# Three edits in a six-stage transformer kernel: local stages with a chain one tick shorter, norms finished in their own tick, half copies on GpSimd, and the distance stage's output made inside its units

## The reference

```python
x = x + 0.5 * _L0_ffn_ref(_layernorm(x), ...)
x = x + _L0_attn_ref(_layernorm(x), ...)        # "distance": softmax(-|q_i - q_j|^2 / sqrt(8)), 16 heads of 8
x = x + 0.5 * _L0_ffn_ref(_layernorm(x), ...)
x = x + 0.5 * _L1_ffn_ref(_layernorm(x), ...)   # "local": 2 layers, below
x = x + _L1_attn_ref(_layernorm(x), ...)        # causal attention, 16 heads of 64
x = x + 0.5 * _L1_ffn_ref(_layernorm(x), ...)   # "local" again
# one local layer (8 heads of 64, windows of 64 rows):
h = shift_token(x)                # columns 64..127 come from the row before
q, k, v = split(h @ wqkv)
q = l2norm(q) * qs; k = l2norm(k) * ksc
q, k = rotary_xpos(q, k)
o = local_attention(q, k, v)      # softmax over own and preceding window, masked
x = x + o @ wo
h = shift_token(x); h = layernorm(h) * lg + lb
a, g = split(h @ w1 + b1)
x = x + (a * gelu(g)) @ w2 + b2
```

## Time and profile before

| | |
|---|---|
| median of 3 runs | 3463.14 us (3461.46 to 3471.44) |
| the profiled execution: time, span | 3464.99 us, 3463.2 us |
| busy in the span: PE, ACT, DVE, POOL | 3167.9 (91%), 2201.9 (64%), 1959.3 (57%), 1441.8 (42%) us |
| distance units, then their output block | 138 to 630 us, 630 to 648 us |
| first local stage | about 729 to 1480 us |
| causal stage between | to about 2700 us |
| second local stage | 2706 to 3463 us |
| granted TensorE clock, mean | 0.971 of 2.4 GHz |

### The profile page before, as it was taken

One profiled execution on the slowest core, in us unless ns is written; L12 is line 12 of the kernel. 1 busy time (PEld: TensorE's weight loads), 2 busy tenths in 40 slices (PEclk: granted clock), 3 DMA queues, 4 the chain that ended last, 5 costly groups with the idle time before them and its releaser, 6 DMA issues. The chain is left out here.

```text
span 3463.2 us, 74421 instructions
## 1 busy us (share of the span) xinstructions
PE 3167.9 (91%) x26438; PEld 1948.0 (56%) x26564; DVE 1959.3 (57%) x4017; ACT 2201.9 (64%) x3837; POOL 1441.8 (42%) x1765
## 2 busy tenths in 40 slices
PE   7799999769999999769999999999999599999996
PEld 5322222436666666546666666666666366666664
DVE  4200000338777777645565655655655587777774
ACT  2599999436766666545555555555555366666664
POOL 1100000037677766423333333333333376777673
PEclk9799999989999999989999999999999799999999
DMA  1122222101111111000000000000000111111111
GB/s 33 30 39 39 36 39 33 67 16 40 35 39 40 39 35 36 21 13 8 6 9 6 9 6 6 9 6 6 9 6 5 25 41 35 38 39 38 37 34 37
DMA packets 121646, 90.38 MB, mean 26 GB/s; under 512 B 79985, under 2 KB 99057, under 8 KB 121329
## 3 DMA queue, kind: packets, MB, share of 16 engines
q1 hardware_dynamic: 121168, 87.70, 11.6%
q10 hardware_dynamic: 288, 0.13, 0.0%
HBM read 17.52 MB, written 2.10 MB: 6 GB/s over the span
## 5 line engine op out<-in xcount | busy, mean ns | idle before, releaser
L1893 POOL TENSOR_SCALAR e<-e,inv 128x768 f32<-128x768 f32 (+7 forms) x512 | 376.8, 749 | 762.0 <-DVE inv L1785 762.0
L1855 ACT ACTIVATE e<-e,nmax 128x768 f32<-128x768 f32 (+7 forms) x512 | 395.6, 773 | 429.4 <-DVE e L1780 426.9
L1780 DVE TENSOR_SCALAR_CACHE_REDUCE e<-slot 128x768 f32<-128x768 f32 (+7 forms) x512 | 376.2, 754 | 247.9 <-PE slot L1669 247.9
L661 ACT ACTIVATE e<-slot 128x1024 f32<-128x1024 f32 x512 | 473.0, 1084 | 15.2 <-PE slot L597 15.2
L998 POOL TENSOR_TENSOR prob<-prob,inv_total 128x1024 f32<-128x1024 f32 x128 | 243.0, 1898 | 319.9 <-DVE inv_total L1377 319.9
L1773 DVE COPY eT<-slot 128x512 f32<-128x512 f32 (+3 forms) x384 | 238.8, 622 | 235.4 <-PE slot L1680 235.3
L1680 PE MATMUL slot<-ident,e 128*128 128x128 f32 x2304 | 333.0, 280 | 8.5 <-DVE eT L1773 3.5
L1663 PE MATMUL slot<-key,q 64*128 64x512 f32 (+3 forms) x1536 | 318.2, 519 | 19.1 <-ACT v L1842 12.8
L1680 PEld LDWEIGHTS slot<-ident,e 128*128 128x128 f32 x2304 | 253.3, 142 | 92.6 <-issue 70.0
L1024 POOL TENSOR_TENSOR rot<-cosine,sine 128x1024 f32<-128x1024 f32 x128 | 302.0, 2360 | 3.8 <-DVE sine L1363 3.8
L1075 PE MATMUL slot<-w_qk,hT 128*128 128x512 f32 x512 | 256.8, 625 | 28.8 <-DVE sine L1363 14.1
(11 more groups left out here) (166 smaller groups left out, 6178.4 us busy)
## 6 DMA issues: line engine op xcount, KB each, us to landing
v_mix<-v SPq DMA_DIRECT2D x256, 128.0 KB, 2.3
w_qkv<-in_causal_w_dram SPq DMA_DIRECT2D x32, 192.0 KB, 2.3
query<-q_hi SPq DMA_DIRECT2D x128, 32.0 KB
keys<-q_hi SPq DMA_DIRECT2D x128, 32.0 KB
query<-q_lo SPq DMA_DIRECT2D x128, 32.0 KB
keys<-q_lo SPq DMA_DIRECT2D x128, 32.0 KB
hs<-H SPq DMA_DIRECT2D x32, 128.0 KB
h1s<-H SPq DMA_DIRECT2D x32, 128.0 KB
```

Source lines behind the costliest of these rows:

```text
L661: act.activation(e[n % E_RING][:], c.slots[n % RING][:].rearrange(flat), ACT.Exp, scale=2 * SCALE).then_inc(e_ready, 1)
L1780: dve.tensor_scalar(e[n % RING][h][:, 0:cols], c.slots[h][:].rearrange(flat)[:, 0:cols], -1.0, None, ALU.mult, ALU.min, accum_out=nmax[:, ...
L1855: act.activation(part, part, ACT.Exp, bias=nmax[:, n, h:h + 1], scale=-1.0, accum_out=total[:, n, h:h + 1]).then_inc(e_ready, 1)
L1893: pool.tensor_scalar(part, part, inv[:, n, h:h + 1], 1.0, ALU.mult, ALU.mult).then_inc(scaled, 1)
```

## The change

Three edits.

1. Local stages: TQ, PT, OT go from 2, 3, 4 to 1, 2, 3. GpSimd makes `inverse_norms` and `unit_rows` for the tick's own tile instead of the tile before, between `floor_norms` and `rotated`, and behind it; ScalarE makes its two operations of `inverse_norms` for the own tile too, behind `heads` (at r = 3 behind `gates(ffn, 2)` and the table load).
2. The unshifted half of `hs` and `h1s` (columns 0 to 63) is no longer a DMA of SyncE but a GpSimd `tensor_copy`: `copy_h1s` at the end of tick r = 0, `copy_hs` at the end of r = 2, each with a semaphore of its own that `row_moments` and `t1` wait for.
3. Distance stage: the output block is gone. `ctx_all` becomes `ctx[half]` for one batch. In the units, TensorE turns a half (`turn_output`) and multiplies it by `wo_eff` (`output`), VectorE copies, adds to X and makes the moments (4 bn_stats, 4 bn_aggr, 1 small copy a half). The block that goes had 8 rounds of 4 transposes, 4 matmuls, 1 ScalarE copy, 1 addition and moments.

In the diff the first `output` is TensorE's, the second VectorE's; `ticks` appears first for GpSimd, then for ScalarE.

```diff
-        ctx_all = sb("ctx_all", [P, NT, P])
+        ctx = [sb(f"ctx{half}", [P, 4, P]) for half in range(2)]
+        cT = sb("cT", [P, 512])
...
+                            if g == 0 and not (isinstance(b, int) and b == 0):
+                                pe.wait_ge(x_ready, 2 * b - 1 + half)
...
+                    def turn_output(b, half):
+                        pe.wait_ge(ctx_ready, 2 * (GROUPS * b + GROUPS - 1) + half + 1)
+                        for t in range(4):
+                            m = pe.transpose(c.slots[3][:, half, t * P:(t + 1) * P], ctx[half][:, t, :], c.ident[:])
+                        m.then_inc(turned, 1)
+
+                    def output(b, half):
+                        pe.wait_ge(cT_ready, 2 * b + half + 1)
+                        for t in range(4):
+                            m = pe.matmul(c.slots[3][:, half, t * P:(t + 1) * P], cT[:, t * P:(t + 1) * P], wo_eff[:],
+                                          start=True, stop=True)
+                        m.then_inc(y_ready, 1)
...
+                            if g == GROUPS - 1 and n == 27:
+                                turn_output(b, 0)
+                            if g == GROUPS - 1 and n == 30:
+                                output(b, 0)
+                            if g == 0 and not first and n == 12:
+                                turn_output(b - 1, 1)
+                            if g == 0 and not first and n == 15:
+                                output(b - 1, 1)
...
+                    def output(b, half):
+                        dve.wait_ge(turned, 2 * b + half + 1)
+                        dve.tensor_copy(cT[:], c.slots[3][:, half, :]).then_inc(cT_ready, 1)
+                        dve.wait_ge(y_ready, 2 * b + half + 1)
+                        xs = c.X[:, bass.ds(b * TPB + 4 * half, 4), :].rearrange("p t d -> p (t d)")
+                        dve.tensor_tensor(xs, c.slots[3][:, half, :], xs, ALU.add).then_inc(x_ready, 1)
...
-    TQ, PT, OT, FFN, DOWN = 2, 3, 4, 2, 3
+    TQ, PT, OT, FFN, DOWN = 1, 2, 3, 2, 3
...
                 def shifted(dst, g, loaded):
-                    sp.dma_start(dst[:, :, 0:64], H[:, bass.ds(row(g), G), 0:64]).then_inc(loaded, 16)
...
+                def same_rows(a, dst, copied):
+                    pool.tensor_copy(dst[:, :, 0:64], H[:, bass.ds(row(a.g), G), 0:64]).then_inc(copied, 1)
...
                         if turned := tile(step, r, PT, depth):
                             scale(turned)
-                        if last := tile(step, r, 1, depth):
-                            inverse_norms(last)
-                            unit_rows(last)
+                        if own := tile(step, r, 0, depth):
+                            floor_norms(own)
+                            inverse_norms(own)
+                            rotated(own)
+                            unit_rows(own)
+                        if r == 0 and (behind := group(step, 2, depth)):
+                            copy_h1s(behind)
+                        if r == 2 and (ahead := group(step, -1, depth)):
+                            copy_hs(ahead)
                         if r == 1 and (ffn := group(step, FFN, depth)):
                             deviations(ffn)
-                        if own := tile(step, r, 0, depth):
-                            floor_norms(own)
-                            rotated(own)
...
-                        if r != 3 and (last := tile(step, r, 1, depth)):
-                            inverse_norms(last)
                         if scored:
                             heads(scored)
                         if r == 3 and ffn:
                             gates(ffn, 2)
                             act.preload_act_table_set("natural_log_exp_and_others")
                         if own:
+                            inverse_norms(own)
                             values(own)
...
-                        if r == 2 and own:
-                            inverse_norms(own)
...
                 def row_moments(a):
-                    dve.wait_ge(h1s_loaded, 80 * a.g + 80)
+                    dve.wait_ge(h1s_loaded, 64 * a.g + 64)
+                    dve.wait_ge(h1s_copied, a.g + 1)
```

More of the change, by code:

```diff
@@ L649, in unit @@
                             turn(b, g, 1)
+                            turn_output(b, 1)
+                            output(b, 1)
                     over_units(pe, unit)
@@ L667, in _ @@
                 def _(dve):
+                    def output(b, half):
[4 more added lines that the diff above has]
+                        dve.tensor_tensor(xs, c.slots[3][:, half, :], xs, ALU.add).then_inc(x_ready, 1)
+                        dve.wait_ge(x_ready, 2 * b + half + 1)
+                        dve.sem_inc(x_seen, 1)
+                        for t in range(4):
+                            dve.bn_stats(x_stats[:, t, :], c.X[:, bass.ds(b * TPB + 4 * half + t, 1), :].rearrange("p t d -> p (t d)"))\
+                               .then_inc(stats_ready, 1)
+                        dve.wait_ge(stats_ready, 4 * (2 * b + half) + 4)
+                        dve.sem_inc(x_seen, 1)
+                        for t in range(4):
+                            dve.bn_aggr(x_means[:, t, :], x_stats[:, t, :]).then_inc(means_ready, 1)
+                        dve.wait_ge(means_ready, 4 * (2 * b + half) + 4)
+                        dve.tensor_copy(c.moments[:, bass.ds(b * TPB + 4 * half, 4), :], x_means[:]).then_inc(moments_ready, 1)
                     def unit(b, g, first=False, last=False):
                         u = GROUPS * b + g
+                        if g == 0 and not first:
+                            output(b - 1, 1)
                         for half in range(2):
@@ L676, in unit @@
                             dve.wait_ge(inv_ready, 2 * u + half + 1)
-                            dst = ctx_all[:, bass.ds(b * TPB + 4 * half, 4), 32 * g:32 * g + 32]
+                            dst = ctx[half][:, :, 32 * g:32 * g + 32]
                             dve.tensor_tensor(dst.rearrange("p t (j d) -> p t j d", d=D), rows[:, :, :, 0:D],
                                               inv[:, half].unsqueeze(3).broadcast_to([P, 4, GROUP, D]), ALU.mult).then_inc(ctx_ready, 1)
+                            if g == GROUPS - 1 and half == 0:
+                                output(b, 0)
@@ L681, in _ @@
+                        if last:
+                            output(b, 1)
                     over_units(dve, unit)
[L682 to L728 removed]
@@ L999, in scale, with copy_hs, copy_h1s @@
                         .then_inc(scaled, 1)
+                def same_rows(a, dst, copied):
+                    pool.tensor_copy(dst[:, :, 0:64], H[:, bass.ds(row(a.g), G), 0:64]).then_inc(copied, 1)
+                def copy_hs(a):
+                    if a.depth:
+                        pool.wait_ge(out_ready, a.g - GROUPS + 1)
+                    else:
+                        pool.wait_ge(h_ready, G * a.g + G)
+                    if known(a.g, 1):
+                        pool.wait_ge(t1_ready, a.g)
+                    same_rows(a, hs, hs_copied)
+                def copy_h1s(a):
+                    pool.wait_ge(h1_ready, G * a.g + G)
+                    if known(a.g, 1):
+                        pool.wait_ge(z_ready, G * a.g)
+                    same_rows(a, h1s, h1s_copied)
                 def deviations(a):
@@ L1056, in _ @@
                 pool.wait_ge(cleared, 4)
+                copy_hs(group(0, 0, None))
                 over_steps(pool, ticks)
```

59 lines of the change are left out of this document (14 added, 45 removed).

## The result

| | before | changed |
|---|---|---|
| median of the runs, us | 3463.64 (3461.46 to 3471.44, 4 runs) | 3582.7 (3573.81 to 3585.03, 4 runs) |
| span of the profiled execution, us | 3463.2 | 3581.7 |
| mean granted clock | 0.971 | 0.962 |
| DMA packets | 121646 | 87853 |

The ratio is 1.0338, 95% interval 1.0319 to 1.0357: slower by 119 us, with 3551 forecast (range 3495 to 3605). The measured time lies 2.7 us above the forecast's own range (3525 to 3580), and the wider one takes it in. The kernel lost where the prediction looked, in the four-tick groups of the two local stages. But the loss in the groups is a third larger than forecast, the drains have the wrong sign, and one thing is at work in most groups that the sum did not contain: the clock.

What follows compares the result with a forecast made beforehand. TensorE, 97% busy, was taken to bound the local stages and be made to wait. Groups 92.3, ramps 12, drains -8.9 and distance output -9.4 sum to +86.0 on 3464.99: 3551 us, range 3495 to 3605.

Steps and rivals of the forecast that it cites:

- Tick 3 to 0: Local stages, `tq` at r = 0: ScalarE's pair stands behind the table load, so TensorE waits 0.75 us.
- Tick 0 to 1 and the copy: Local stages: no wait of `tq`; `copy_h1s` takes 0.4 us, `row_moments` follows it and VectorE's queue is 1.2 late.
- Tick 1 to 2: Local stages, `tq` at r = 2: late `totals` delays `scale` and the 8.3 us chain; 2.25 us late in all.
- t3: Local stages, tick 2: z comes after `deviations`, `scale`, `floor_norms`, the pair and `v`; `t3` is 3.8 us late in all.
- The 0.45 back from `hidden`: Each local-stage group: a pair ahead of the Gelu table load goes, taking nearly all of `qk`'s 0.5 us wait.
- The group, 3.35: Four ticks of a local stage: 3.8 - 0.45 = 3.35 us longer; 92.3 us over two stages.
- Rival C: Local-stage groups: VectorE's lateness feeds on itself, or the clock; 5 us a group, +132, 3597 us; chance 0.12.
- The ramp, 12: Start of each local stage: the chain bounds the tick and `tq` stands ahead of other work; 6 us a stage.
- The drain, -8.9: End of each local stage: VectorE's DMA waits of 1.99 and 6.88 us both go.
- The distance output, -9.4: Distance stage: the tail falls from 17.5 to 4.5 us (-12.9), insertions in the units cost 3.5.
- Rival A: Local stages: the chain hides and TensorE keeps its pace; -31, 3434 us; chance 0.09.
- Rival B: Local stages: only the chain to `tq` bites, `t3` does not; 1.8 us a group, +43, 3508 us; chance 0.20.

Runs made afterwards that it cites:

- dev_first: Changed kernel with GpSimd's four `deviations` moved from the end of tick 1 to its head, ahead of `scale`; 3534.86 us.
- dev_cen_first: Changed kernel with GpSimd's `deviations` at the head of tick 1 and ScalarE's z ahead of the pair and v of tick 2; 3520.5 us.
- fill16: Changed kernel with sixteen transposes of the identity put on TensorE ahead of `t3`, in the wait for z; 3556.07 us.
- short_scale: Changed kernel with GpSimd's `scale` on 8 of the 128 columns of a head, order and semaphores unchanged; 3487.21 us.
- undo2: Changed kernel with only the second edit taken back: DMAs bring all parts of `hs` and `h1s`, GpSimd copies nothing; 3568.38 us.
- short_unit: Changed kernel with GpSimd's `unit_rows` on 4 of the 64 columns of a head, order and semaphores unchanged; 3478.03 us.

## Why the prediction was right, and where its sizes were off

The mechanism was right: TensorE, the bound, is made to wait for GpSimd's chain at r = 0 and 2 and for z at r = 2. By the spans the forecast fell short by 32.5 us, 31 of them in the groups; the other misses nearly cancel, and that they do is luck. The terms, forecast and measured between the two spans:

| term | forecast | measured |
|---|---|---|
| groups, 28 | 92.3 | 123.5 |
| ramps | 12 | 9.1 |
| drains | -8.9 | +5.0 |
| distance output | -9.4 | -8.6 |
| elsewhere ahead of the first stage | 0 | -6.8 |
| between the stages | 0 | -3.7 |
| sum | 86.0 | 118.5 |

**Tick 3 to 0**: 0.75 forecast, 0.66 and 0.67 measured. Right.

**Tick 0 to 1 and the copy**: no wait of `tq`, and `copy_h1s` takes 0.40, as its bound said; the statistics wait 0.40 for it. Right. But its price over the kernel was counted in the chain's alone; the copies cost 6.2 us even where the chain is the old one.

**Tick 1 to 2**: 2.25 late in all was forecast. The two waits add up to 0.66 + 1.65 = 2.31. Right.

**t3**: 3.8 late in all was forecast. By its start `t3` is 4.04 late: 28.68 us behind the group's first squares (1042.62), where it was 24.64 (1055.98 less 1031.34). Mis-sized by a quarter of a microsecond. The waits add up to more, 4.69, since the smaller ones of the old order are gone, chiefly the 0.28 for H and 0.25 of the projection of the values at 1052.21. The order of the causes, deviations behind `unit_rows` and z behind the next `scale`, is what `dev_first` and `dev_cen_first` bear out.

**The 0.45 back from `hidden`**: the wait is gone (0.2 us in all where the earlier trace rows had one in each group). Right; but `qk`'s was one of three small waits that stood in each group, and the sum left out the other two.

**The group, 3.35**: by the squares most groups are 3.7 to 5.0 longer (47.6 to 48.0 against 42.8 to 44.1), 123.5 / 28 = 4.4 on the mean. The step that failed is this sum: it added the waits and left everything behind them at its old length. `t3`, `pt` and `up` take 0.42, 0.88 and 0.33 longer at the low clock. In `fill16`, where the clock stays full and the chain is the same, the groups of both stages are 92.9 us longer than before (by the squares, the ramps taken off as above), against 92.3 forecast. So the waits were priced right, and the clock, priced at nothing, is the other 31; for the whole kernel `fill16` measured it at 26.6. Rival C named the clock, beside VectorE's lateness, at 5 us a group and a chance of 0.12; the clock half of it is what happened, at 1.1 us on the mean and not at 1.65. The Trainium skill, "TensorE: Matmul & The Clock Gate", Part 1, has the clock follow how busy TensorE has lately been. The trace agrees: 1.00 at 97% busy, 0.97 at 90.54, and the fall stands behind the longest wait of the group in nine of eleven groups and goes when that wait is filled.

**The ramp, 12**: the squares of tiles 0 and 7 stand 65.4 and 64.5 apart in the two stages, 60.7 and 60.0 before: 9.1. Well within its ends.

**The drain, -8.9**: here the sign was wrong. Both of VectorE's waits for the DMA did come off the end, as forecast: the last statistics stand without a wait at 1516.39 and 3555.91. The step that failed is that what lies ahead of them in the drain was left at its old length. The drain's ticks hold the chain too. TensorE in the first drain, whose last squares are at 1460.16:

```profile
1470.92 1.97 PE L1132 MATMUL slot<-ident,rot 128*128 128x128 f32 x8 [1.70 <-POOL rot L1008]
...
1485.09 1.97 PE L1160 MATMUL slot<-ident,prob 128*128 128x128 f32 x8 [2.55 <-POOL prob L1015]
...
1493.31 1.11 PE L1197 MATMUL slot<-ident,z 128*128 128x128 f32 x4 [0.39 <-DVE H L1420]
1495.29 6.72 PE L1210 MATMUL slot<-zT,w 128*128 128x512 f32 x8 [0.87 <-ACT zT L1329]
```

and before, with the last squares at 1410.24:

```profile
1438.24 0.63 PE L1156 MATMUL slot<-ident,z 128*128 128x128 f32 x4 [0.47 <-DVE H L1382]
...
1440.21 3.60 PE L1169 MATMUL slot<-zT,w 128*128 128x512 f32 x8
```

The last `tq` waits 1.70 for the unit rows, the last `pt` 2.55 for `scale`, and the clock falls behind both (1.97 us each, where they take 1.09 before):

```profile
1485.00:1505.00 20.00, 15.28 (x64) 9.02 (x64) 1.79 (x3) 6.59 (x10) 2.09 (x6) 0.59 0.03 7
```

So `t3` of the last group but one starts 33.15 us behind the last squares, where it was 28.00, and 33.56 in the second stage: 10.7 in both. From there to the last statistics the second stage gains 7.1, its DMA wait of 6.88 and a little; the first loses 0.9, since `up` takes 6.72 in place of 3.60 at the low clock and so spends more than the DMA's 1.99. Behind them lie another 0.5 and 0. That is 10.7 - 7.1 + 0.9 + 0.5 = 5.0. `short_scale` bears it out for the way to `t3`: with `scale` short the last `pt` waits 0.96 and 1.27, and `t3` stands 29.17 and 29.82 behind the last squares. In the first drain `up` then takes 3.70 and the drain 77.0; in the second the clock is low at `t3` too (`up` 5.38, that of the last group 6.42 where the changed kernel has 5.09), and the drain, 69.5, is only 0.7 shorter than the changed kernel's. How much of the 10.7 is waiting and how much the clock, no run separates.

**The distance output, -9.4**: the tail was forecast at 4.5, and it takes 5.1, from 627.42 + 0.29 to 632.67 + 0.17 (timeline of VectorE, beside the earlier trace rows):

```profile
627.42 0.29 DVE L736 TENSOR_TENSOR ctx<-slot,inv 128x128 f32<-128x128 f32 x1
...
632.67 0.17 DVE L722 COPY moments<-x_means 128x8 f32<-128x8 f32 x1
```

So the tail gained 12.3, where 12.9 was forecast. The insertions into the units were forecast at 3.5, and from the second context to the last the trace has 450.73 us, where it had 447.03: 3.7. That this is so near is in part luck. The intervals between contexts that hold twelve of the fourteen insertions are 5.9 us longer together (0.49 each, not 0.25), and the one in the middle (357 to 390 us), which holds the other two, is 2.2 shorter, which cannot be the edit's alone: over the kernels with the same units it varies from 31.8 to 36.7 us. The two parts make -8.6, near the forecast. The 12.2 of the medians (its interval is 7 to 17) and the 15.4 ahead of the first local stage have more in them: 5.9 of the 15.4 lie ahead of the second context, where the code is the same and the granted clock of 100 to 200 us is 0.92 against 0.85, and 0.9 behind the last moments.

**The margins.** Rival A fell: GpSimd is busy for 66.57 of 100 us and the chain bites all the same, since it is its place in the tick and not its load that counts. Rival B fell with the wait for z.

## What to carry to other kernels

Before a result is asked for one tick earlier, lay every link between its first input and its use end to end, on all engines and in each queue's order, and compare that with the tick; an engine that is a third idle can still be the one that is waited for, and where two branches meet, shortening one shows only the difference to the other. Do the same for what fills and empties the pipeline: the drain's ticks held the chain's waits too. Where the bound is TensorE, give a new wait two prices: its own length, and, as a rival with a chance of its own, the operations behind it at half the clock. What a copy or a move costs depends on the slack of the queue that it is put in: the same copies cost 6 us where there was slack and 14 where the chain was tight.

## What the runs showed of the hardware

- In a TensorE that was otherwise busy the granted clock fell behind nine of ten waits of 2.3 to 2.4 us that recurred every 47.7 us, each some 6.7 us behind another of 1.6 to 1.8 (0.72 over 1070 to 1076, 1.00 from 1076 to 1090). A fall cost about 1.3 us.
- With a first wait of 1.1 and a second of 2.4 (`undo2`, 990 to 1220 us) it fell in three of five groups; with waits of 0.6 to 0.7 and 2.1 to 2.4 us some 21 us apart and none for z (`dev_cen_first`) in 3 of 13 groups of the first stage (0.96 over such a group); with one of 1.6 for z (`short_unit`) it stayed at 1.00 over 530 us. No run shows what decides between falling and not.
- Sixteen transposes that compute nothing, put into the wait of 2.4 us, held the clock at 1.00 over 530 us and made the kernel 26.6 us faster.
- GpSimd's long operations kept their length wherever they were moved beside VectorE: `scale` and `unit_rows` took 1.896 and 1.901 us on the mean of 128 each, 1.898 and 1.904 before.
